# Moving the first shared expert from the routing stage to the opening of linear attention, and the folded latent weights to the opening of the first dense layer

## The reference

```python
x = x + 0.5 * routed_ffn(layernorm(x))       # 64 experts, 6 of them per token, and a shared expert
x = x + gated_linear_attention(layernorm(x)) # 8 heads, keys of 128, values of 32
x = x + 0.5 * routed_ffn(layernorm(x))       # the same weights again
x = x + 0.5 * dense_ffn(layernorm(x))        # all 8 experts computed, gates of the best 2
x = x + latent_attention(layernorm(x))       # 16 heads, latent of 64
x = x + 0.5 * dense_ffn(layernorm(x))
```

```python
shared = silu(x @ Sg.T) * (x @ Su.T) @ Sd.T  # Sg, Su: 352 x 256, Sd: 256 x 352
# latent attention: queries x @ W_q (16 heads of 128), keys and values latent @ W_kv_up, output @ W_o
# the kernel folds W_q with W_kv_up ("absorb") and W_kv_up with W_o ("mix") once, before the layer
```

## Time and profile before

| | |
|---|---|
| three timed runs | 1664.99, 1667.15 (median), 1667.41 us |
| profiled execution | 1674.61 us, its span 1672.9 us |
| busy in the span | PE 1440.8 us (86%), DVE 1083.4 (65%), POOL 771.9 (46%), ACT 756.0 (45%) |
| route 0 | 6.3 to 125.2 us |
| routed experts 0 | 125.2 to 278.5 us |
| opening of linear attention, to the first `scale(0, 0)` | 281.2 to 356.5 us |
| dense layer 0 begins | 930.4 us |

### The profile page before, as it was taken

How to read it: one execution, slowest core, us unless ns; L and a number is a source line. 1 busy time by engine, 2 the same in 40 slices (tenths; PEclk the granted TensorE clock), 3 DMA queues, 4 the chain that set the end, 5 groups by cost and what they waited for, 6 DMA issues and landing times. The chain is left out here.

```text
span 1672.9 us, 39408 instructions
## 1 busy us (share of the span) xinstructions
PE 1440.8 (86%) x14334; PEld 995.1 (59%) x14334; DVE 1083.4 (65%) x2759; ACT 756.0 (45%) x1786; POOL 771.9 (46%) x741
## 2 busy tenths in 40 slices
PE   6879996647898996888999388878999999998898
PEld 3556664424555654455666266645677777776687
DVE  6852222577775654783222487958889898884898
ACT  5534443345556533643444211226766666662322
POOL 4454333754410000554333575408889888892000
PEclk9989998669899997989999688989999999999899
DMA  8309996421100002503998232100000000000000
GB/s 268 99 10 262 309 317 184 143 73 48 51 17 1 1 1 70 167 26 122 298 315 246 82 103 77 57 1 15 3 16 4 15 5 3 16 3 3 10 22 20
DMA packets 92677, 145.63 MB, mean 87 GB/s; under 512 B 25032, under 2 KB 52528, under 8 KB 92512
## 3 DMA queue, kind: packets, MB, share of 16 engines
q1 hardware_dynamic: 62816, 93.06, 18.9%
q0 software_dynamic: 15360, 37.77, 7.6%
q10 hardware_dynamic: 14336, 12.59, 2.8%
HBM read 122.39 MB, written 18.87 MB: 84 GB/s over the span
## 5 line engine op out<-in xcount | busy, mean ns | idle before, releaser
L2308 POOL TENSOR_TENSOR sb_m_prob<-sb_m_prob,sb_m_rinv 128x512 f32<-128x512 f32 x256 | 259.9, 1041 | 50.6 <-DVE sb_m_rinv L2358 46.2
L1273 POOL DMA_INDIRECT sb_c_rows<-slot_rows,sb_slot x192 | 190.4, 992 | 95.5 <-issue 52.3
L2238 ACT ACTIVATE sb_m_prob<-m_ps_s,sb_m_nmax 128x512 f32<-128x512 f32 x256 | 173.6, 683 | 131.2 <-DVE sb_m_nmax L2364 129.7
L1106 POOL DMA_INDIRECT e_xn<-xn_rows,sb_table x128 | 117.7, 919 | 180.7 <-PE e_ps_x L1185 168.5
L1256 DVE TENSOR_TENSOR sb_e_h<-sb_e_sg,e_ps_gu 96x176 f32<-96x176 f32 x128 | 42.6, 333 | 226.8 <-ACT sb_e_sg L1232 226.8
L2364 DVE TENSOR_REDUCE sb_m_nmax<-m_ps_s 128x1 f32<-128x512 f32 x256 | 164.0, 682 | 23.3 <-PE m_ps_s L2142 21.4
L1194 PE MATMUL e_ps_gu<-e_wgu,sb_e_xT 128*96 128x352 f32 x512 | 172.9, 460 | 0.5 <-ACT sb_e_xT L1226 0.5
L2372 DVE STREAM_TRANSPOSE sb_m_pT<-sb_m_prob 128x1024 f32<-128x1024 f32 x128 | 157.6, 1233 | 0.0
L2141 PE MATMUL m_ps_s<-sb_m_latT_high,sb_m_qa 128*128 128x512 f32 x256 | 128.1, 500 | 14.5 <-ACT sb_m_prob L2238 13.9
L2155 PE MATMUL m_ps_v<-sb_m_pT,sb_m_lat_rows 32*64 32x128 f32 x8192 | 135.6, 274 | 5.1 <-issue 5.0
L2155 PEld LDWEIGHTS m_ps_v<-sb_m_pT,sb_m_lat_rows 32*64 32x64 f32 x8192 | 119.2, 130 | 29.0 <-issue 28.6
(11 more groups left out here) (280 smaller groups left out, 3109.6 us busy)
## 6 DMA issues: line engine op xcount, KB each, us to landing
e_wgu<-wgu SPq DMA_DIRECT2D x128, 352.0 KB, 6.9
e_wdn<-wdn SPq DMA_DIRECT2D x128, 192.0 KB, 6.3
slot_rows<-sb_e_y ACTq DMA_DIRECT2D x128, 96.0 KB, 6.2
xn_rows<-e_xn SPq DMA_DIRECT2D x16, 256.0 KB, 2.2
sb_c_rows<-slot_rows,sb_slot POOLq DMA_INDIRECT x192, 2.8
sb_x<-x SPq DMA_DIRECT2D x4, 512.0 KB, 5.5
e_xn<-xn_rows,sb_table POOLq DMA_INDIRECT x128, 6.6
sb_g_zm<-wqT SPq DMA_DIRECT2D x1, 2048.0 KB, 9.1
```

Source lines behind the costliest of these rows:

```text
L1106: pool.indirect_dma_start(x, None, k.xn_rows[:, :], bass.IndirectOffsetOnAxis(ap=k.table[:, e:e + 1], axis=0))\
L1273: pool.indirect_dma_start(rows[u][j][:, :], None, k.slot_rows[:, :], bass.IndirectOffsetOnAxis(ap=k.slot[:, n, j:j + 1], axis=0))\
L2238: act.activation(prob[s % 4][:, hh, :], ps_s[j % 3][:, :], ACT.Exp, bias=nmax[s % 2][:, hh:hh + 1], accum_out=rsum[s % 2][:, hh:hh + 1]).t ...
L2308: pool.tensor_tensor(part, part, rinv[s % 2][:, hh:hh + 1].to_broadcast([P, T]), ALU.mult)\
```

## The change

Four things are done.

1. The shared expert of route 0 is taken out of `route` (the guard `shared = r == 1`; route 1 keeps it). The transposed normalised tokens of route 0 are kept in `xnT0`, which lives until linear attention.
2. `linear_attention` computes it. PE does `gate_up` 0, 1, `down(0)`, `gate_up(2)`, `down(1)` before its first transposes, and `gate_up(3)`, `down(2)`, `down(3)` in slot -1. ACT copies and applies Silu, with the reload of the activation table after group 2 and again after group 3. The products are now all DVE's (`hidden`), and the statistics of tiles 0 and 1 come behind the sum of group 0.
3. The folds go to the opening of `dense_experts` 0: four before the first transposes and four behind the first logits, into the banks `ps_e`, with ACT copying. Their weights are loaded by SP at the end of `routed_experts` 1, and the gathered rows of the dense layer now use the weight buffers of the experts.
4. The constant `chunk_keep` and its two memsets are dropped, and in linear attention POOL issues the first gathers ahead of the five memsets of `same_head`.

```diff
@@ route
+    shared = r == 1
-            pe.wait_ge(k.sem("w0_ffn_loaded"), 16 * 4)
-                if m % 2 and m < NPR:
+                if shared and m % 2 and m < NPR:
                     gate_up(q, 1)
...
@@ linear_attention, tensor
+            def gate_up(q):
+                for c, (m0, rows) in enumerate(MSC):
+                    if q or c:
+                        pe.wait_ge(gu_copied, 3 * q + c)
+                    for which in range(2):
+                        for d in range(DC):
+                            ins = pe.matmul(ps_o[which][0:rows, :], k.sguT[:, d, which * MS + m0:which * MS + m0 + rows],
+                                            xnT[:, d, q * QT:(q + 1) * QT], start=(d == 0), stop=(d == DC - 1))
+                    ins.then_inc(gu_ready, 1)
+
+            def down(q):
+                pe.wait_ge(hid_ready, 2 * (q + 1))
+                for half in range(2):
+                    if q:
+                        pe.wait_ge(down_used, 2 * q + half - 1)
...
+                if u == -1:
+                    gate_up(3)
+                    down(2)
+                    down(3)
...
+            gate_up(0)
+            gate_up(1)
+            down(0)
+            gate_up(2)
+            down(1)
             pe.wait_ge(k.sem("w0_loaded"), W0)
-            pe.wait_ge(made, 1 + HG)
             pe.wait_ge(w_high, 2)
-            pe.wait_ge(raw_loaded, 48)
-            for n in range(FOLDS):
-                fold(n)
@@ linear_attention, vector
                 if u == -2:
+                    hidden(2)
+                    shared_added(1, 0)
+                    shared_added(1, 1)
                     add_rows(4, range(TOPK))
...
+                if u == -1:
+                    shared_added(3, 0)
+                    shared_added(3, 1)
                 add_rows(n, range(4))
...
                 edges(u + 2)
+                if u == -2:
+                    hidden(3)
+                    shared_added(2, 0)
+                    shared_added(2, 1)
...
-            for n in range(TB):
+            hidden(0)
+            add_rows(0, range(TOPK))
+            add_rows(1, range(TOPK))
+            hidden(1)
+            dve.wait_ge(k.sem("c_rows_added"), 2 * TOPK)
+            shared_added(0, 0)
+            shared_added(0, 1)
+            dve.wait_ge(down_used, 1)
+            statistics(0)
+            statistics(1)
+            for n in range(2, TB):
@@ dense_experts, tensor
+            if combine is not None:
+                pe.wait_ge(raw_loaded, 48)
+                for n in range(ABSORBS):
+                    fold(n)
             transposed(0, 0)
             logits(0, 0)
+            if combine is not None:
+                for n in range(ABSORBS, FOLDS):
+                    fold(n)
+                pe.wait_ge(fold_free, FOLDS)
             pe.wait_ge(we_low, (r + 1) * DC)
             tiles(pe, tile)
```

More of the change, by code:

```diff
@@ L245, in dense_experts @@
         if combine is not None:
-            rows = [[sb(f"c{combine}_rows{u}_{j}", [P, D]) for j in range(TOPK)] for u in range(3)]
+            places = [buffer[:, c, 0:D] for buffer in k.wgu for c in range(DC)]
+            rows = [places[u * TOPK:(u + 1) * TOPK] for u in range(3)]
         ps_x = ps(f"d{r}_ps_x", [P, DC, P])
@@ L364, in _ @@
             if combine is not None:
+                for n in range(ABSORBS):
+                    fold_copy(n)
                 inverse_deviation(0, 0)
@@ L745, in _ @@
                         down(q - 1, 1)
-                if m % 2 == 0:
+                if shared and m % 2 == 0:
                     if q < NQ:
@@ L831, in _ @@
                     tokens(m - 1)
-                if m % 2:
+                if shared and m % 2:
                     gate_up_copies(q, 1)
@@ L896, in _ @@
                     places(m - 1)
-            last_hidden()
+            if shared:
+                last_hidden()
             k.pool_steps = s.n
@@ L1084, in _ @@
             slots(f, n_capped)
-            for half in range(2):
-                shared_added(NQ - 1, half)
+            if shared:
+                for half in range(2):
+                    shared_added(NQ - 1, half)
             k.dve_steps = s.n
@@ L1791, in _ @@
             pool.sem_inc(k.sem("c_rows_used"), 2)
+            for n in range(2 * TB):
+                gather(n)
             pool.memset(same_head[:, :], 0.0).then_inc(made, 1)
@@ L1796, in _ @@
             pool.wait_ge(made, 1 + HG)
-            for n in range(2 * TB):
-                gather(n)
             for u in range(-1, U):
@@ L1807, in _, with hidden, shared_added @@
             s = Counted(dve, dve_steps, 0)
+            def hidden(q):
+                for c, (part, rows) in enumerate(((slice(0, 2), P), (slice(2, 3), MSC[2][1]))):
+                    dve.wait_ge(silu_ready, 2 * q + c + 1)
+                    gated = sgate[q % 2][0:rows, part, :]
+                    dve.tensor_tensor(gated, gated, sup[q % 2][0:rows, part, :], ALU.mult).then_inc(hid_ready, 1)
+            def shared_added(q, half):
+                dve.wait_ge(down_ready, 2 * q + half + 1)
+                x = k.X[:, TB * q + 2 * half:TB * q + 2 * half + 2, :]
+                dve.scalar_tensor_tensor(out=x, in0=ps_down[half], scalar=0.5, in1=x, op0=ALU.mult, op1=ALU.add)\
+                   .then_inc(down_used, 1)
             def add_rows(n, js):
                 if n < NT:
+                    if n >= 2 and 0 in js:
+                        dve.wait_ge(down_used, n // 2 + 1)
                     for j in js:
```

206 lines of the change are left out of this document (121 added, 85 removed).

## The result

Over 20 executions each, the kernel before has a median of 1667.2 us (1664.6 to 1676.1) and the kernel after 1674.0 us (1671.3 to 1678.0). The ratio is 1.0037, with a 95% interval of 1.0028 to 1.0046: 0.37% slower, 6.8 us by the medians. Single executions differ by up to 11 us, so one profile does not measure this. The profiled execution of after has a span of 1672.3 us and that of before 1672.9; each kernel was therefore profiled once more (the first two rows of the experiments). The table is worked out from the two profiles of each; a stage ends where the next begins.

A forecast was written before the change was run, and what follows sets the result against it. It took route 0's steps as set by the shared expert's matmuls and casts held by POOL, and linear attention's opening by POOL's gathers. Terms -15.7 and +23.5 gave +7.8 us on 1667.15: 1675, range 1657 to 1683.

The forecast's parts named there:

- Six held casts in route 0: Route 0, steps 1 to 6: DVE's cast held until POOL's comparison ends, 10.85 us a step; route 0 gains 15.0 us.
- the mark: Route 0: the end of `posf` on DVE, once per step, from which the forecast counted; 12.5 us apart in the kernel before.
- Stage end: End of route 0: set by POOL's fourth gather instead of DVE's last shared addition, a gain of 1.9 us.
- Cold start of the routed experts: Routed stage behind route 0: PE's first 512-column instructions start cold, 1.5 us more.
- `chunk_keep`: Its memset on POOL before a barrier is dropped: 0.3 us less, between 0 and 0.6.
- Opening of linear attention: Up to `scale(0, 0)`: tile 2's gather starts 17.5 us later, waiting for `down(0)`; the stretch +23.5 us in sum.
- The two DVE groups: Opening of linear attention: `hidden(2)` and `hidden(3)`, each with two additions on DVE, 3.3 us each, +6.6 us.
- Folds: Opening of the dense layer: the moved folds stay hidden there, as in their old place; 0 us.
- rival B: Route 0, steps 5 and 6: the cast gets ahead of POOL's comparison; 6.7 us less, 1668, no change; chance 0.22.
- C: Rival, route 0: the cast is free in all six steps; 20.1 us less, 1655, faster; chance 0.18.
- D: Rival, dense layer: the folds come onto the path; +5.9 us, 1681; chance 0.15.
- PEclk would read near 0.5 in route 0: Sign expected in the profile after: PE at the half clock in route 0, without the 512-column matmuls.

The follow-up runs named there:

- The delayed kernel: The kernel after with two extra 64-column products on PE ahead of the logits of steps 5 and 6 of route 0: 1682.1 us (one execution).
- the warmed kernel: The kernel after with eight more 512-column matmuls on PE behind the last table matmul of route 0: 1676.1 us, ratio 1.0055 to before.
- The bank experiment: The kernel after with two pairs of PSUM banks for `gate_up` of groups 0 to 2 in linear attention's opening: 1666.2 us, ratio 0.9987 to before.
- the cast kernel: The kernel after with DVE's cast of the experts' numbers written as an addition of a zero in PSUM: 1664.1 us, ratio 0.9976 to before.

## Why the prediction came out right, point by point

- **Six held casts in route 0: wrong by two.** "So I count six held steps" is the step that failed, and in it that the logits "end some 0.3 to 0.5 us too late". The rule was right (a row maximum later than about 1.5 us behind the mark pushes the cast into the comparison), and so was PE's pace (1.95 us of logits), though not its reason, since the clock column reads 1.00. But transposes, table and logits together ended sooner than I had put them, 1.21 us behind the mark; the prediction shows no rows for that sum. The row maximum started 1.44 behind the mark, inside the limit by 0.14 us at the cast. The delayed kernel shows the other side, 6.2 us. Four held and two free steps are 43.2 + 15.4 + 7.2 = 65.8 us against the forecast's 72.6, and the table's cast came 22.5 us earlier in the means.
- **Stage end: mis-sized,** -0.5 and not -1.9. PE starts 2.2 us behind POOL's last gather (101.75 against 99.57), where I had ended the stage with the gather's issue. The transfers move until about 101.0, so its landing seems to count too; no run tests it.
- **Cold start of the routed experts: right in kind,** 2.4 and not 1.5; the warmed kernel's 156.0 shows it. `chunk_keep`, 0.3 us, can't be told from the rest.
- **Opening of linear attention: right,** +25.2 against +24.1. Tile 2's gather was 17.9 later (17.5 forecast) for the reason given: bank and copy cycle of 4.88 (4.94), `down(0)` done 34.9 behind the start (33.9). The bank experiment moves it with the cycle, to 28.6. The two DVE groups were taken at 3.3 us each and are 1.81 + 0.68 + 0.68 = 3.2.
- **Folds: right,** 0, by the kernel with them alone: its interval leaves at most 3 us.
- **What hid the miss:** route 0 and the stages to linear attention gave 5 us more than forecast (-20.6 against -15.7 to that stage's start), the closing layer took 3 back, and the opening and the rest of linear attention 1 each. That these nearly cancel is luck. Without the stop (3 to 4 us) the kernel after would have come near 1670 (worked out, not run), at the edge of what can be told from no change and nearer to rival B. The forecast named neither the stop nor the row that could have shown it: no row of the kernel before has it.
- **Rivals.** B happened, as a part, and with PE slow: not by the fast PE that the forecast gave as one way to it. C did not by itself; its condition, all casts free, was made in the cast kernel and gave 10 us (1664) beside the two steps that were free already, in steps of 8.2 us and not 7.5. D did not. The forecast's sign that PEclk would read near 0.5 in route 0 was wrong, though the durations were slow.

## What to carry to other kernels

When work leaves an engine that set a step's length, look for locks that lay beside it: removing the held casts gave the kernel before nothing and the kernel after 10 us. And look at what stands behind a held instruction: where that can be held too, freeing the first only moves the wait, as the product in steps 2 and 4 shows. Where a term hangs on a start time within a few tenths of a microsecond, give both outcomes and look for what moves the edge. Work moved out of a waiting place into the head of a chain with a short ring delays every later link: order the release first, and double the banks, before judging the move. A change of a few instructions early in a program can cost microseconds in a loop far behind it, so compare the untouched stages too.

## What the runs showed of the hardware

- A jump back over 301 DVE instructions cost nothing in three programs (four profiles) and 3.3 to 4.2 us in nine others (ten profiles); 17 instructions more, ahead of it, made the difference. The total of queue q14 is 4 to 6 packets higher with the stop.
- DVE's cast of 128x12 from uint32 to f32 within SBUF is held by POOL's tensor instruction (2.77 us); the addition of a PSUM operand, with the same input and output in SBUF, is not (0.17 us). DVE's product of two SBUF tensors, 96x512 in f32, is held too: 2.96 us instead of 0.68.
- 34 waits for x that were fulfilled by 6.6 us at the latest (the start of DVE's statistics in the kernel before), held in 17 instructions, put DVE's first instruction 1.6 us later (7.96 against 6.30 and 6.39) and the first `posf` 2 to 3 us.
